# A smaller first sort in single steps, and expert chunks of three, two and three tiles, in a transformer block with mixture of experts

## The chip, the cores and the metric

The kernel runs on one core of a Trainium2 chip. The metric is the device time of one execution in microseconds (us). A core has a tensor engine (PE, with its weight loads PEld), a vector engine (DVE), a scalar engine (ACT), a general engine (POOL) and a sync engine (SP). Each runs its own instructions in order and waits on semaphores; transfers are issued on the queues of SP, ACT and POOL.

## The reference

The input is 8 sequences of 512 tokens with 256 channels. Causal attention with 16 heads of 16 channels is followed by a residual sum and a layer norm, and this by a mixture of 8 experts in which each expert picks tokens, and again by a residual sum and a layer norm. Cut to what matters here:

```python
x = _layernorm(x + attn(x))
# experts: capacity = 512 * 2 / 8 + 1 = 129
scores = softmax(einsum('bsd,ed->bse', x, router_w), axis=-1)
gate_vals, sel_idx = top_k(swapaxes(scores, 1, 2), capacity)   # per sequence and expert
tokens = x[b_idx, sel_idx]
h = gelu(einsum('becd,edh->bech', tokens, w1) + b1)            # 256 -> 1024
y = einsum('bech,ehd->becd', h, w2) + b2                       # 1024 -> 256
out = zeros_like(x).at[b_idx, sel_idx].add(y * gate_vals[..., None])
x = _layernorm(x + out)
```

So each pair of sequence and expert has 129 tokens: 128, which make one tile (numbered as its sequence), and one over. The leftover tokens of all 8 sequences make a tile of 8 rows, called LEFT.

## The kernel before

**Attention.** `steps()` (L105) is one list of stages in an order written out by hand; every engine walks through it and does its own part. It counts iterations i from -3 to 8 (B = 8), each with 40 places (four groups g of ten, place = 10 g + k). Iteration i does the scores and exponentials (`st`) of sequence i; the products for the row maxima (`nat`) run some three quarters of an iteration ahead, those of values (`av`) a quarter behind; projection, layer norm and router logits (`onorm`, `ot`, `proj`, `rstd`, `logit`, `lexp`, `x1`, `score`) run for the sequence before; `qk` and `v` prepare the sequence after next. DVE reduces the `nat` tiles (L522), which go round three PSUM banks, and other stages share two banks (`stage_ps`), so that PE waits for DVE where DVE is late. Iteration 8 holds only the end of sequence 7.

**First sort.** A sequence and an expert are one row of 512 scores. EARLY = 6 sequences give 48 rows. `pick` (PE transposes, DVE copies to `row_pool`, L592) stands at place 1 of iteration 7. `pick_round` (L149) finds the eight largest of each row, their places, and strikes them out: three DVE operations (MAX8 L152, FIND_INDEX8 L153, MATCH_REPLACE8 L155), each waited for by the next. 17 rounds find 129 values. ROUND_AT puts 13 rounds in iteration 7 and 4 in iteration 8, the last at place 16. `picked` (place 17) casts the places to float (L597), transposes them (L738) and adds the sequences' bases (L601); `fetch` on POOL gathers the tokens of expert jobs 0 and 1 (L424). `cut` (iteration 8, places 1 and 12) splits the first expert's two weights in a high part (ACT, L451) and a low part (POOL, L417). The experts' phase begins when all engines have ended attention.

**Experts.** The tiles are grouped in CHUNKS: (0, 1, 2), (3, 4, 5), (6, 7, LEFT), with 384, 384 and 264 columns. A job is an expert and a chunk; there are 24, in the order of JOBS: (0,0), (0,1), (1,0), (1,1), (0,2), (1,2), then expert by expert, and for the last expert chunk 2 first. `expert_steps()` (L794) is again one list for all engines. Iteration q has ten places m: the eight `up` units of job q + 1 (six matmuls each, L1152), and the `down` tiles of job q (24 matmuls each, L1166) at m = 2, 5, 8. ACT makes gelu (L1021) and the high part (L1026), DVE the low part h_lo (L1090; for job 0 POOL, L979). For a down tile DVE makes y in two operations (L1101, L1104), and POOL adds it to `acc` in memory with an indirect transfer (L993). `turn` of job q + 2 (m = 6) transposes gathered tokens (PE L1128, ACT L1012, DVE tt_lo L1064); `fetch` of job q + 3 (m = 5) gathers them (POOL L962). `cut1` and `cut2` split the next expert's weights (ACT L1034, POOL L985): for expert 1 in iteration 0 at m = 3 and 4; for experts 3 to 7 at m = 1 and 4 of the iteration two before their first job.

**Second sort.** The remaining sequences (LATE = 2, 16 rows) are sorted by DVE in 17 rounds over the iterations -1, 0 and 1 (5, 6 and 6 rounds, same `pick_round`); `picked` at (2, 3) makes their token numbers and those of LEFT (L1079, L1081); the gather of job 4 waits for them.

**End.** FINISH lists at which (q, m) a sequence of `acc` is loaded (SP, L942) and normalized (`norm`: DVE L1109 to L1115, POOL L999, L1001). In this list a stage of place m comes ahead of the down of the same place. ACT applies the norm (L1044) and issues the store (L1037).

Of the kernel before, what the change touches and what calls it, by code (L numbers as in the profile page):

```python
# [5 lines left out]
F32 = mybir.dt.float32  # L6
F32R = mybir.dt.float32r
# [7 lines left out]
P = 128  # L15
# [4 lines left out]
KC = C // P  # L20
# [84 lines left out]
def steps():  # L105

    for i in range(-3, B + 1):
# [40 lines left out]

def pick_round(nc, link, pool, best, at, r):  # L149

    src, eight = pool[r % 2], slice(8 * r, 8 * r + 8)
    link(nc.vector.max(best[:, eight], src[:, :]))  # L152
    link(nc.vector.max_index(at[:, eight], best[:, eight], src[:, :]))  # L153
    if r + 1 < ROUNDS:
        link(nc.vector.match_replace(pool[(r + 1) % 2][:, :], best[:, eight], src[:, :], -1.0))  # L155
# [9 lines left out]
def attention(nc, ctx, xt_d, x_d, wqkv_d, wp_d, wpn_d, rw_d, x1_d, acc_d, ident, scores, chosen, w1_d, w2_d, ahead):  # L165
# [328 lines left out]
    def _(dve):  # L494
# [11 lines left out]
        for stage, b, n in steps():  # L506
# [87 lines left out]
            elif stage == "round":  # L594
                pick_round(nc, link, row_pool, best, best_at, n)
                if n == ROUNDS - 1:
                    nc.vector.tensor_copy(best_f[:, :], best_at[:, :]).then_inc(best_ready, 1)  # L597
# [147 lines left out]
CHUNKS = ((0, 1, 2), (3, 4, 5), (6, 7, LEFT))  # L745
NC = len(CHUNKS)
LATE = B - EARLY
# [11 lines left out]
DOWN_AT = (2, 5, 8)  # L759


def rows_of(tile):
    return B if tile == LEFT else P


def job(q):
# [27 lines left out]
def expert_steps():  # L794
# [4 lines left out]
    for q in range(-1, NQ):  # L799
        for m in range(KH + 2):  # L800
# [18 lines left out]
            if q >= 0 and m in DOWN_AT:  # L819
                yield "down", q, m // 3  # L820
# [18 lines left out]
def experts(nc, ctx, x1_d, acc_d, w1_d, b1_d, w2_d, b2_d, out_d, ident, scores, chosen, ahead):  # L839
# [21 lines left out]
    tok = [ahead["tok0"], ahead["tok1"]] + [sb(f"tok{n}", [P, 3, C], F32) for n in range(2, TOK_RING)]  # L861
    tt_hi = sb("tt_hi", [P, TOK_RING, KC, 3 * P], F32R)
    tt_lo = sb("tt_lo", [P, TOK_RING, KC, 3 * P], F32R)
    g = sb("g", [P, G_RING, 3 * P], F32)
    h_hi = sb("h_hi", [P, 2, KH, 3 * P], F32R)
    h_lo = sb("h_lo", [P, 2, KH, 3 * P], F32R)
# [84 lines left out]
    def _(pool):  # L951
# [17 lines left out]
        for stage, q, n in expert_steps():  # L969
            if stage == "fetch":  # L970
                gather(q)
            elif stage == "up" and q < LO_BY_POOL:
# [3 lines left out]
                if q >= 2 and n == 0:  # L976
                    pool.wait_ge(y_done, 3 * (q - 1))
# [8 lines left out]
            elif stage == "down":  # L986
                e, tiles, _ = job(q)
                j = tiles[n]
                pool.wait_ge(y_ready, 3 * q + n + 1)
# [14 lines left out]
    def _(act):  # L1004
        for stage, q, n in expert_steps():
# [7 lines left out]
            elif stage == "up":  # L1013
# [9 lines left out]
                if q >= 2 and n == 0:  # L1023
                    act.wait_ge(y_done, 3 * (q - 1))
                act.wait_ge(g_done, at + 1)
                nc.scalar.activation(h_hi[:, q % 2, n, 0:cols], g[:, at % G_RING, 0:cols], ACT.Copy).then_inc(g_hi, 1)  # L1026
            elif stage in ("cut1", "cut2"):
# [3 lines left out]
                elif q >= 2:  # L1031
                    act.wait_ge(y_done, 3 * (LAST_JOB[q - 2] + 1))
# [18 lines left out]
    def _(dve):  # L1051
# [7 lines left out]
        for stage, q, n in expert_steps():  # L1059
# [22 lines left out]
            elif stage == "up" and q >= LO_BY_POOL:  # L1082
                _, _, cols = job(q)
                at = KH * q + n
                if q >= 2 and n == 0:
                    dve.wait_ge(y_done, 3 * (q - 1))
# [5 lines left out]
            elif stage == "down":  # L1092
                e, tiles, _ = job(q)
                j, at = tiles[n], 3 * q + n
# [23 lines left out]
    def _(pe):  # L1118
        for stage, q, n in expert_steps():
            e, tiles, cols = job(q) if stage in ("turn", "up", "down") else (0, (), 0)  # L1120
            if stage == "turn":
                pe.wait_ge(tok_in[q % TOK_RING], 48 * (q // TOK_RING + 1))
# [32 lines left out]
            elif stage == "down":  # L1155
                at, rows = 3 * q + n, rows_of(tiles[n])
# [14 lines left out]
def build(nc, xt_d, x_d, wqkv_d, wp_d, wpn_d, rw_d, w1_d, b1_d, w2_d, b2_d, out_d):  # L1171
    x1_d = nc.dram_tensor("x1", [B * T, C], F32).ap()
    acc_d = nc.dram_tensor("acc", [B * T, C], F32).ap()
    with ExitStack() as both:
        def sb(name, shape, dt):
# [14 lines left out]
            "tok0": sb("tok0", [P, 3, C], F32),  # L1190
            "tok1": sb("tok1", [P, 3, C], F32),
# [43 lines left out]
```

## Time and profile before

| | before |
|---|---|
| median of 3 runs | 968.44 us (965.9 to 968.86) |
| the profiled execution | 968.14 us, its span 966.2 us |
| PE busy | 833.6 us (86%), 5864 matmuls |
| DVE busy | 649.0 us (67%) |
| ACT busy | 534.6 us (55%) |
| POOL busy | 527.7 us (55%) |
| transfers | 100.51 MB, mean 104 GB/s |

Busy time is what the engine's own instructions cover; it doesn't say what sets the end. The span of the profiled execution is from its first to its last recorded instruction; the time is somewhat longer. "Idle before" is an engine's idle time ahead of a group and what ended it. Waits give who was waited for; "issue" is time in which an engine waited for nothing that the profile shows. The chain that ended last follows the work back from the last instruction. PEclk or the clock column is the share of full speed (2.4 GHz) that TensorE was granted: 1.00 is full, 0.5 the lower level (1.2 GHz), values between are means over a stretch with both. Attention fills the first 493 us or so, the experts the rest.

### The profile page before, as it was taken

The numbers are of one execution on the slowest core, as the hardware profiler recorded it, in microseconds if no ns is written. First come the engines' busy times: TensorE is split into PE (matmuls) and PEld (weight loads), VectorE is DVE, ScalarE is ACT, GpSimd is POOL, SyncE is SP. The second block draws the span as 40 slices with busy tenths as digits, with TensorE's granted clock in tenths as the row PEclk, the third lists the DMA queues.
The fourth block names the chain that finished last, engine by engine and source line by source line (L and its number), as shares of the span: only waits on it lengthen the run. The fifth ranks groups of instructions, "written<-read, shape, count | busy, mean of one in ns | idle before, by whom it ended". The sixth has DMA issues, their size and how long they took to land. (4 is left out here: it accounts for less than half of the span.)

```text
span 966.2 us, 17052 instructions
## 1 busy us (share of the span) xinstructions
PE 833.6 (86%) x5864; PEld 623.9 (65%) x5864; DVE 649.0 (67%) x1985; ACT 534.6 (55%) x1042; POOL 527.7 (55%) x639
## 2 busy tenths in 40 slices
PE   4669999999999999977656899998989899898990
PEld 3434454544545453433356889998989899898990
DVE  4467778787877878999749955555464735547454
ACT  2126667667676766645345345564555556455455
POOL 6336665656565653323645247757375645738343
PEclk9768999999999999988879899999999999999995
DMA  4998778877776869100151324325242332422257
GB/s 142 165 151 134 123 121 144 144 144 143 141 147 112 153 99 205 62 24 20 47 202 53 74 40 82 96 38 137 35 126 45 93 63 47 125 34 35 37 132 250
DMA packets 90101, 100.51 MB, mean 104 GB/s; under 512 B 8736, under 2 KB 83488, under 8 KB 89888
## 3 DMA queue, kind: packets, MB, share of 16 engines
q1 hardware_dynamic: 72560, 77.92, 38.3%
q0 software_dynamic: 12800, 16.92, 10.3%
q10 hardware_dynamic: 4656, 4.59, 1.4%
q8 instruction: 47, 0.77, 0.3%
q14 instruction: 38, 0.31, 0.1%
HBM read 65.38 MB, written 33.62 MB: 102 GB/s over the span
## 5 line engine op out<-in xcount | busy, mean ns | idle before, releaser
L522 DVE CUSTOM_DVE_ANT_0 n_ps<-n_ps,tri 128x512 f32<-128x512 f32 (+3 forms) x512 | 238.8, 519 | 86.0 <-PE n_ps L652 84.3
L438 ACT ACTIVATE pt<-st_ps 128x512 f32<-128x512 f32 x320 | 184.3, 602 | 68.4 <-PE st_ps L637 53.2
L1090 DVE TENSOR_TENSOR h_lo<-g,h_hi 128x384 fp32r<-128x384 f32 (+1 forms) x184 | 132.6, 729 | 125.5 <-ACT h_hi L1026 116.3
L1166 PE MATMUL y_ps<-w_parts,h_hi 128*128 128x256 f32 (+1 forms) x1152 | 212.4, 279 | 0.3 <-ACT h_hi L1026 0.3
L1021 ACT ACTIVATE g<-h_ps,b 128x384 f32<-128x384 f32 (+1 forms) x192 | 104.3, 543 | 193.5 <-PE h_ps L1152 159.3
L1152 PE MATMUL h_ps<-tt_hi,w_parts 128*128 128x384 f32 (+1 forms) x768 | 177.3, 335 | 30.6 <-issue 20.0
L381 POOL TENSOR_SCALAR_AFFINE_SELECT pt<-pt 128x256 f32<-128x256 f32 (+1 forms) x320 | 110.7, 363 | 125.3 <-ACT pt L438 124.5
L1166 PEld LDWEIGHTS y_ps<-w_parts,h_hi 128*128 128x128 f32 (+1 forms) x1152 | 171.6, 177 | 3.6 <-ACT h_hi L1026 0.6
L993 POOL DMA_INDIRECT acc<-y,tok_no x64 | 103.7, 1621 | 114.7 <-DVE y L1104 105.9
L1166 PE MATMUL y_ps<-w_parts,h_lo 128*128 128x256 f32 (+1 forms) x576 | 160.6, 279 | 0.0
L1152 PEld LDWEIGHTS h_ps<-tt_hi,w_parts 128*128 128x128 f32 x768 | 132.2, 198 | 33.4 <-issue 31.8
L637 PE MATMUL st_ps<-w_parts 99*128 99x512 bf16 (+3 forms) x512 | 126.9, 310 | 16.8 <-ACT pt L438 14.8
L652 PE MATMUL n_ps<-w_parts 96*128 96x512 bf16 (+3 forms) x512 | 127.0, 312 | 11.2 <-DVE nmax L522 7.5
L1166 PEld LDWEIGHTS y_ps<-w_parts,h_lo 128*128 128x128 f32 (+1 forms) x576 | 101.8, 177 | 2.0
L637 PEld LDWEIGHTS st_ps<-w_parts 99*128 99x128 bf16 x512 | 41.8, 99 | 89.6 <-ACT pt L438 56.9
L1026 ACT ACTIVATE h_hi<-g 128x384 fp32r<-128x384 f32 (+1 forms) x192 | 94.4, 492 | 7.4
L669 PE MATMUL av_ps<-pt,vaug 128*32 128x512 f32 (+3 forms) x1024 | 97.1, 454 | 1.6 <-POOL pt L381 1.6
L1152 PE MATMUL h_ps<-tt_lo,w_parts 128*128 128x384 f32 (+1 forms) x384 | 95.5, 332 | 0.0
L962 POOL DMA_INDIRECT tok<-x,tok_no x58 | 58.9, 1015 | 33.0 <-DVE left_no L1081 16.4
L985 POOL TENSOR_TENSOR w_parts<-w_raw,w_parts 128x2048 fp32r<-128x2048 f32 x14 | 67.5, 4868 | 12.8 <-ACT w_parts L1034 12.8
L522 DVE DVE_READ_ACCUMULATOR2_ANT nmax<- 128x1 f32 x512 | 72.8, 142 | 0.0
L652 PEld LDWEIGHTS n_ps<-w_parts 96*128 96x128 bf16 x512 | 44.7, 100 | 41.9 <-DVE nmax L522 26.2
(160 smaller groups left out, 1137.6 us busy)
## 6 DMA issues: line engine op xcount, KB each, us to landing
w_parts<-part_d SPq DMA_DIRECT2D x192, 128.0 KB, 6.5
w_raw<-in_w SPq DMA_DIRECT2D x16, 1024.0 KB
part_d<-w_raw SPq DMA_DIRECT2D x96, 128.0 KB, 6.6
w_raw<-in_xt SPq DMA_DIRECT2D x8, 512.0 KB, 4.7
res<-in_x SPq DMA_DIRECT2D x8, 512.0 KB, 10.4
x<-res SPq DMA_DIRECT2D x8, 512.0 KB, 3.3
acc<-res SPq DMA_DIRECT2D x8, 512.0 KB, 4.7
fin<-acc SPq DMA_DIRECT2D x4, 512.0 KB, 4.2
```

What stands on the lines that cost most here:

```text
L381: nc.gpsimd.affine_select(out=x, in_=x, compare_op=ALU.is_ge, fill=0.0, base=0, pattern=[[0, len(tiles)], [1, P]], channel_multiplier=-1). ...
L438: nc.scalar.activation(pt[:, slot % PT_RING, n % UP, :], st_ps[at % ST_RING][:, :], ACT.Exp, scale=S_SCALE).then_inc(exp_done, 1)
L522: ins = nc.vector.tensor_tensor_reduce(out=src[:, h, :], in0=src[:, h, :], in1=mask, scale=-1.0, scalar=-BIG_NEG, op0=ALU.add, op1=ALU.min ...
L637: ins = nc.tensor.matmul(st_ps[at % ST_RING][:, c:c + T - kb * P], kst[0:KM, b % 2, h, kb * P:(kb + 1) * P], qst[0:KM, b % 2, h, kb * P:T] ...
L652: ins = nc.tensor.matmul(bank[:, j * w:(j + 1) * w], qst[0:KQ, b % 2, h, qb * P:(qb + 1) * P], kst[0:KQ, b % 2, h, 0:w], start=True, stop= ...
L669: ins = nc.tensor.matmul(av_ps[VW * j:VW * (j + 1), n * P:T], vaug[:, seq % 3, n, h, :], pt[:, (seq * PAIRS + h // 2) % PT_RING, u, c:c + ...
L993: nc.gpsimd.indirect_dma_start(acc_d[:, :], bass.IndirectOffsetOnAxis(ap=choice(e, j), axis=0), y[0:rows_of(j), j, :], None, compute_op=AL ...
L1021: nc.scalar.activation(g[:, at % G_RING, 0:cols], h_ps[at % H_RING][:, 0:cols], ACT.Gelu, bias=b1[:, e, n:n + 1]).then_inc(g_done, 1)
L1026: nc.scalar.activation(h_hi[:, q % 2, n, 0:cols], g[:, at % G_RING, 0:cols], ACT.Copy).then_inc(g_hi, 1)
L1090: nc.vector.tensor_tensor(h_lo[:, q % 2, n, 0:cols], g[:, at % G_RING, 0:cols], h_hi[:, q % 2, n, 0:cols].bitcast(F32), ALU.subtract).then ...
L1152: ins = nc.tensor.matmul(h_ps[at % H_RING][:, 0:cols], w[e % 2][:, k, units], x[:, q % TOK_RING, k, 0:cols], start=i == 0, stop=i == len(t ...
L1166: ins = nc.tensor.matmul(y_ps[at % Y_RING][0:rows, 0:C], x[:, q % 2, m, toks], w[e % 2][:, m, :], start=i == 0, stop=i == len(terms) - 1)
```

## The change

EARLY falls from 6 to 5: the first sort has 40 rows and can start one iteration earlier, at place 1 of iteration 6. Its 50 operations (the last round needs no strike-out) are no longer placed in rounds of three but one by one (`sort_step`): eight in iteration 6 (every fifth place from 3 on), in iteration 7 one at places 2, 4, 7 and 9 and from place 10 one in each place, two where the place divides by 4. That makes 49; the last one stands at place 9 of iteration 8, where `picked` and `fetch` now are (before: place 17). The `cut` places stay.

The second sort therefore has LATE = 3 sequences, 24 rows. The middle chunk must hold sorted sequences only, so CHUNKS becomes (0, 1, 2), (3, 4), (5, 6, 7, LEFT), with 384, 256 and 392 columns. Downs stand at m = 3, 7 for a chunk of two tiles, at 2, 5, 8 for three and at 1, 4, 7, 9 for four. Waits that counted three tiles per job count with `downs_before` and `gathered`. JOBS, the cuts, the rounds of the second sort, `turn` and `fetch` places stay. FINISH is written anew: sequences 6, 7 and 5 are loaded in the last iteration but one; 3 and 4 come last.

```diff
-EARLY = 6
+EARLY = 5
 ROUNDS = -(-CAP // 8)
 CUTS_AT = ((B, 1), (B, 12))
-ROUND_AT = [(B - 1, place) for place in (1, 2, 8, 11, 12, 16, 17, 23, 25, 26, 32, 38, 39)]
-ROUND_AT += [(B, place) for place in (1, 5, 12, 16)]
+PICKED = (B, 9)
+SORTS = 3 * ROUNDS - 1
+SORT_AT = {(B - 2, place): 1 for place in range(3, 40, 5)}
+SORT_AT.update({(B - 1, place): 1 for place in (2, 4, 7, 9)})
+SORT_AT.update({(B - 1, place): 1 + (place % 4 == 0) for place in range(10, 40)})
...
-                if (i, place) == (B - 1, 1):
+                if (i, place) == (EARLY + 1, 1):
                     yield "pick", 0, 0
-                if (i, place) in ROUND_AT:
-                    yield "round", 0, ROUND_AT.index((i, place))
+                for n in range(SORT_AT.get((i, place), 0)):
+                    if sorts < SORTS:
+                        yield "sort", 0, sorts
+                        sorts += 1
                 if (i, place) in CUTS_AT:
                     yield "cut", 0, CUTS_AT.index((i, place))
-                if (i, place) == (B, 17):
+                if (i, place) == PICKED:
+                    while sorts < SORTS:
+                        yield "sort", 0, sorts
+                        sorts += 1
                     yield "picked", 0, 0
                     yield "fetch", 0, 0
...
+def sort_step(nc, link, pool, best, at, n):
+
+    r, what = n // 3, n % 3
+    src, eight = pool[r % 2], slice(8 * r, 8 * r + 8)
+    if what == 0:
+        link(nc.vector.max(best[:, eight], src[:, :]))
+    elif what == 1:
+        link(nc.vector.max_index(at[:, eight], best[:, eight], src[:, :]))
+    else:
+        link(nc.vector.match_replace(pool[(r + 1) % 2][:, :], best[:, eight], src[:, :], -1.0))
...
-CHUNKS = ((0, 1, 2), (3, 4, 5), (6, 7, LEFT))
+CHUNKS = ((0, 1, 2), (3, 4), (5, 6, 7, LEFT))
...
-DOWN_AT = (2, 5, 8)
+DOWN_AT = {2: (3, 7), 3: (2, 5, 8), 4: (1, 4, 7, 9)}
...
+def downs_before(q):
+
+    return sum(len(CHUNKS[c]) for _, c in JOBS[:q])
...
-FINISH = [((NQ - 2, 0), "load", 6), ((NQ - 2, 1), "load", 7), ((NQ - 2, 4), "norm", 6), ((NQ - 2, 7), "norm", 7),
-          ((NQ - 1, 0), "load", 0), ((NQ - 1, 1), "load", 1), ((NQ - 1, 3), "load", 2), ((NQ - 1, 4), "norm", 0),
-          ((NQ - 1, 5), "load", 3), ((NQ - 1, 8), "load", 4), ((NQ - 1, 9), "load", 5)]
-FINISH += [((NQ - 1, 9), "norm", b) for b in range(1, 6)]
+FINISH = [((NQ - 2, 1), "load", 6), ((NQ - 2, 2), "load", 7), ((NQ - 2, 3), "load", 5), ((NQ - 2, 5), "norm", 6), ((NQ - 2, 7), "norm", 7),
+          ((NQ - 2, 9), "norm", 5), ((NQ - 1, 0), "load", 0), ((NQ - 1, 1), "load", 1), ((NQ - 1, 3), "load", 2), ((NQ - 1, 4), "norm", 0),
+          ((NQ - 1, 5), "norm", 1), ((NQ - 1, 7), "norm", 2), ((NQ - 1, 8), "load", 3), ((NQ - 1, 9), "load", 4)]
+FINISH += [((NQ - 1, 9), "norm", b) for b in (3, 4)]
...
-            if q >= 0 and m in DOWN_AT:
-                yield "down", q, m // 3
+            if q >= 0 and m in DOWN_AT[len(CHUNKS[JOBS[q][1]])]:
+                yield "down", q, DOWN_AT[len(CHUNKS[JOBS[q][1]])].index(m)
```

## Rows read from the trace of the kernel before

**Rows 1.** Busy time by stage: stretch, length, each engine's busy time (x instructions), clock, DMA

```profile
388.00:412.00 24.00, 22.79 (x168) 10.65 (x167) 22.85 (x104) 16.09 (x31) 9.27 (x25) 1.00 0.15 48
...
412.00:453.00 41.00, 31.13 (x203) 13.76 (x201) 37.72 (x120) 19.77 (x36) 12.24 (x33) 0.88 0.04 14
```

**Rows 2.** Waits of PE, 412 to 466 us: who waited for whom, total, times, longest

```profile
PE st_ps L637 <- ACT pt L438: 5.1, 5, 3.4
...
PE n_ps L652 <- DVE nmax L522: 3.2, 2, 1.9
...
PE stage_ps L714 <- DVE nm L555: 1.8, 1, 1.8
```

**Rows 3.** Groups of DVE instructions, 412 to 466 us: busy, mean ns | idle before

```profile
L152 DVE MAX8 best<-row_pool 48x8 f32<-48x512 f32 x15 | 10.2, 682 | 0.3
```

**Rows 4.** Timeline, end of attention: start, length, engine, line, tile, shapes [idle before]

```profile
465.79 9.02 POOL L417 TENSOR_TENSOR w_parts<-w_raw,w_parts 128x2048 fp32r<-128x2048 f32 x2 [1.40 <-ACT w_parts L451]
...
472.73 2.17 DVE L597 CAST best_f<-best_at 48x136 f32<-48x136 uint32 x1
...
482.81 0.94 POOL L424 DMA_INDIRECT tok<-x,tok_no  x1 [0.30 <-issue]
...
483.77 1.06 POOL L410 TENSOR_TENSOR rstd<-ve,half 128x4 f32<-128x4 f32 x1
```

**Rows 5.** Chain that ended last, 490 to 625 us: start, length, what

```profile
522.01 8.35 DVE h_lo L1090
...
554.23 1.15 issue
...
564.66 0.07 DVE left_no L1081
...
570.48 1.11 PE tp_ps L1128 x6
...
623.01 0.99 issue
```

**Rows 6.** Chain that ended last, 636 to 700 us, one expert's period

```profile
642.09 2.16 PE h_ps L1152 x18
...
644.25 2.80 PE y_ps L1166 x24
...
656.93 3.52 issue
...
660.45 4.94 PE h_ps L1152 x18
...
668.19 3.13 PE h_ps L1152 x18
```

**Rows 7.** Timelines of POOL and DVE in that period

```profile
646.56 4.62 POOL L985 TENSOR_TENSOR w_parts<-w_raw,w_parts 128x2048 fp32r<-128x2048 f32 x1 [1.76 <-ACT w_parts L1034]
...
653.79 5.13 POOL L985 TENSOR_TENSOR w_parts<-w_raw,w_parts 128x2048 fp32r<-128x2048 f32 x1
...
653.60 5.48 DVE L1104 TENSOR_SCALAR y<-y,gate 128x256 f32<-128x256 f32 x1
```

**Rows 8.** Chain that ended last, 860 to 967 us

```profile
880.40 2.84 issue
...
917.15 3.13 PE h_ps L1152 x18
...
944.12 6.16 DMA acc<-y,tok_no
...
950.30 6.89 DMA w_raw<-acc
...
957.22 1.42 DVE stats L1109 x4
```

**Rows 9.** All 72 additions: from the instruction's start to landing, from the source view of L993

```profile
DMA to landing us min/median/max: 2.6/3.8/3.9
```

**Rows 10.** The page, part 6: a load of the sum, KB each, median us to landing

```profile
fin<-acc SPq DMA_DIRECT2D x4, 512.0 KB, 4.2
```

More of the change, by code:

```diff
@@ L105, in steps @@
 def steps():
+    sorts = 0
     for i in range(-3, B + 1):
@@ L146, in numbers @@
     return {x: n for n, x in enumerate(x for x in steps() if x[0] in stages)}
-def pick_round(nc, link, pool, best, at, r):
[L151 to L155, printed above, removed]
+def sort_step(nc, link, pool, best, at, n):
[7 more added lines that the diff above has]
+        link(nc.vector.match_replace(pool[(r + 1) % 2][:, :], best[:, eight], src[:, :], -1.0))
+def pick_round(nc, link, pool, best, at, r):
+    for n in range(3 * r, min(3 * r + 3, SORTS)):
+        sort_step(nc, link, pool, best, at, n)
 def weight_parts(ahead, name, slot):
@@ L593, in _ @@
                 dve.wait_ge(dve_free, dve_no[(stage, b, n)] + 1)
-            elif stage == "round":
-                pick_round(nc, link, row_pool, best, best_at, n)
-                if n == ROUNDS - 1:
+            elif stage == "sort":
+                sort_step(nc, link, row_pool, best, best_at, n)
+                if n == SORTS - 1:
                     nc.vector.tensor_copy(best_f[:, :], best_at[:, :]).then_inc(best_ready, 1)
@@ L744 @@
 LEFT = B
-CHUNKS = ((0, 1, 2), (3, 4, 5), (6, 7, LEFT))
+CHUNKS = ((0, 1, 2), (3, 4), (5, 6, 7, LEFT))
 NC = len(CHUNKS)
+TILES = max(len(chunk) for chunk in CHUNKS)
+WIDE = 3 * P + B
 LATE = B - EARLY
@@ L758, with gathered @@
 ROUNDS_IN = (5, 6, 6)
-DOWN_AT = (2, 5, 8)
+DOWN_AT = {2: (3, 7), 3: (2, 5, 8), 4: (1, 4, 7, 9)}
 def rows_of(tile):
     return B if tile == LEFT else P
+def downs_before(q):
+    return sum(len(CHUNKS[c]) for _, c in JOBS[:q])
+def gathered(q):
+    return 16 * sum(len(CHUNKS[JOBS[x][1]]) for x in range(q % TOK_RING, q + 1, TOK_RING))
 def job(q):
@@ L860, in experts @@
     w2_hi, w2_lo = zip(*(weight_parts(ahead, "w2", slot) for slot in range(2)))
[L861 to L866, printed above, removed]
+    tok = [ahead["tok0"], ahead["tok1"]] + [sb(f"tok{n}", [P, TILES, C], F32) for n in range(2, TOK_RING)]
+    tt_hi = sb("tt_hi", [P, TOK_RING, KC, WIDE], F32R)
+    tt_lo = sb("tt_lo", [P, TOK_RING, KC, WIDE], F32R)
+    g = sb("g", [P, G_RING, WIDE], F32)
+    h_hi = sb("h_hi", [P, 2, KH, WIDE], F32R)
+    h_lo = sb("h_lo", [P, 2, KH, WIDE], F32R)
     y = sb("y", [P, B + 1, C], F32)
@@ L976, in _ @@
                 if q >= 2 and n == 0:
-                    pool.wait_ge(y_done, 3 * (q - 1))
+                    pool.wait_ge(y_done, downs_before(q - 1))
                 pool.wait_ge(g_hi, at + 1)
@@ L1023, in _ @@
                 if q >= 2 and n == 0:
-                    act.wait_ge(y_done, 3 * (q - 1))
+                    act.wait_ge(y_done, downs_before(q - 1))
                 act.wait_ge(g_done, at + 1)
@@ L1085, in _ @@
                 if q >= 2 and n == 0:
-                    dve.wait_ge(y_done, 3 * (q - 1))
+                    dve.wait_ge(y_done, downs_before(q - 1))
                 if q == LO_BY_POOL and n == 0:
@@ L1093, in _ @@
                 e, tiles, _ = job(q)
-                j, at = tiles[n], 3 * q + n
+                j, at = tiles[n], downs_before(q) + n
                 rows, before = rows_of(j), sum(j in CHUNKS[c] for _, c in JOBS[:q])
@@ L1121, in _ @@
             if stage == "turn":
-                pe.wait_ge(tok_in[q % TOK_RING], 48 * (q // TOK_RING + 1))
+                pe.wait_ge(tok_in[q % TOK_RING], gathered(q))
                 for k in range(KC):
@@ L1155, in _ @@
             elif stage == "down":
-                at, rows = 3 * q + n, rows_of(tiles[n])
+                at, rows = downs_before(q) + n, rows_of(tiles[n])
                 if n == 0:
@@ L1189, in build @@
             "w2_raw": sb("w2_raw", [P, KH, C], F32),
-            "tok0": sb("tok0", [P, 3, C], F32),
-            "tok1": sb("tok1", [P, 3, C], F32),
+            "tok0": sb("tok0", [P, TILES, C], F32),
+            "tok1": sb("tok1", [P, TILES, C], F32),
             "w1": sb("w1_parts", [P, 2, 2 * KC * HID], F32),
```

4 lines of the change are left out of this document (2 added, 2 removed).

## Prediction

> **What bounds the kernel now.** I read the page first: TensorE is the busiest engine, fuller in the second half (the experts) than around the seam of the two phases. Then busy time by stage. From 388 us on both engines are full: 22.79 us of PE and 22.85 of DVE in 24 us [rows 1]. From 412 to 453 us, where the last sequence is started and the first sort runs, DVE has 37.72 of 41 us, PE only 31.13, at a mean granted clock of 0.88 [rows 1]. PE's waits say for whom: 3.2 us in two waits and 1.8 us in one for DVE directly, and 3.4 us in one wait for an ACT that itself waits for the last router logits, which stand behind sort rounds on DVE [rows 2]. So DVE bounds this stretch. At the seam a chain over DVE and POOL decides: the cast that ends the sort lasts 2.17 us beside the weight cuts on POOL, and the variance step on POOL starts when six gathers are out, at 483.77 us [rows 4].
>
> The chain that ended last tells of the experts. Early on it runs through DVE (the late sort, and one h_lo of 8.35 us beside two cuts) [rows 5]. Later it is PE all the way, broken once in each expert's period: PE stands 3.52 us, and its next 18 matmuls take 4.94 us, not 3.13 [rows 6]. The timelines show why: the second cut (5.13 us on POOL) holds a DVE operation for 5.48 us [rows 7], and the low parts of the next turned tokens are queued behind it. The end is a chain of addition, load, normalization and store, with 6.16 and 6.89 us for the two transfers [rows 8].
>
> **The change, part by part.** I count against the profiled execution: 968.14 us, span 966.2, so 1.9 us lie around the span; it stands 0.3 us under the median of 968.44. One sort step (MAX8, FIND_INDEX8 or MATCH_REPLACE8 with its value load) is about 0.76 us: 682 ns and the gap [rows 3]. I price it alike for 40 and 48 rows, and the late sort alike for 24 and 16, since each partition holds one row.
>
> *Sort in attention.* There are 50 steps either way. Before, 39 stand in the last sequence and 11 behind it; now 8 stand in the sequence before, 41 in the last, 1 behind. Ahead of the last logits, up to where DVE decides, are 8 + 25 steps instead of 30: 3 more, 2.3 us. The copy of the rows (about a step) is moved, not added. The first half of sequence 6 can take some of it; its second half has 1.15 us idle in 24 [rows 1]. Against that, three rounds in the first quarter of the last sequence become four single steps, so DVE's idle 3.3 us in 412 to 453 [rows 1], when it waits for a slowed PE, should mostly go. I take -1.5 us. Bounds: +6.8 (eight steps and the copy all on the path) and -8.4 (all three waits above go [rows 2]).
>
> *Seam.* Ten of the steps behind the last sequence leave the projections' way. What is late next is POOL. The cast now comes beside the first cut, which begins at 465.79 and takes half of 9.02 us [rows 4], so it ends near 470.5; then transposes, and gathers from 471.9; five at 1.25 us to 478.1; then the second cut, now queued behind them, 4.5 us to 482.7; then the variance step, 1.0 us ahead of 483.77 [rows 4]. The last projection's DVE steps may run beside that cut; no row shows their kind there, so the bounds are +3 (held to its end) and -5. The Trainium skill ("SBUF — State Buffer", Who interferes with whom) says that an instruction with at most one SBUF input, outside the two-port modes, is not held by GpSimd. By it the -1.0 stands; if all were held it would be +3. No run yet shows it.
>
> *Start of the experts.* Jobs 0 to 3 are now 3, 2, 3, 2 tiles. DVE has the same 17 rounds in iterations -1 to 1 and still decides; it saves one y in iteration 1 and a third of the columns in two jobs, by estimate three sort steps' worth, 2.2 us. PE's matmuls are equal in sum (1032 columns, nine tiles per expert) but come later: two jobs whose 48 up matmuls take 5.6 instead of 8.35 us (0.117 each, from 2.80 for 24 [rows 6]) and one down of 2.80 us less get done by the end of iteration 2, so 8.3 us of work are left over. Iteration 2 gets no shorter: tiles 5 to 7 and the leftover must be picked before job 4 is gathered. From the leftover's number (564.7) to the transposes (570.48) it took 5.8 us [rows 5]; with a fourth gather it is 7.0, and PE has some 3 us less to do meanwhile. I put 0.1 us. Sum -2.2 + 8.3 + 0.1 = +6.2; bounds +3 (iteration 2 shortens by its work) and +9.
>
> *Second expert's cut.* It falls beside a four-tile job with two downs after the turn, so the 0.99 us stall [rows 5] and 0.2 us of slow clock go: -1.2 (0 if not).
>
> *The cuts of experts 3 to 7.* Both stand in the iteration with the middle chunk's downs and the last chunk's ups. Let it begin at 0 (642.09 us). Before: PE is out of work at 14.8, the second cut starts at 11.7, and PE gets its tokens at 18.4 [rows 6, 7]. After: two ups of 1.065 us (3.13 / 3 for 384 columns [rows 6]) instead of 0.72 stand ahead of the first cut, +0.7. The first down is a place later, behind one more h_lo that this cut holds, and its addition stands ahead of the second cut on POOL: +0.5, of which I keep 0.3. Tokens at 19.4; PE again out of work at 14.8 (8 x 1.065, 0.7 for the turn, 2 x 2.80). The stall grows by 1.0 in four periods. In the fifth, whose stall was 2.84 [rows 8], by 1.7. PE then runs slow: behind 3.52 us of standing that cost 1.8 [rows 6]; I add 0.5 for each, an estimate. Sum 4.0 + 1.7 + 2.5 = +8.2; bounds 0 (no growth) and +13.
>
> *End.* The last job has two tiles and no ups beside it. In DVE's order the normalization of sequence 2 now stands ahead of the last y. Counted from the start of iteration 22: tile 2's matmuls end at 14.0; behind a normalization on DVE and its power step on POOL its addition goes out at 16.9, lands 3.8 us later [rows 9], the load 4.2 later [rows 10], near 25; with 2.1 us of statistics (1.42 of them sums [rows 8]) the last y comes at 27 and its addition at 29.2, though PE ended at 19.6. Then 3.8 to the load, about 5 for it (between 4.2 [rows 10] and 6.89 [rows 8]), 9.0 as before: 47. Before it was 49.05 (from 917.15 [rows 8]), but 5.55 us of PE work have moved ahead of this point: +3.5; bounds -4.3 (DVE doesn't wait) and +7.7 (both transfers as slow as before).
>
> Sum: -1.5 - 1.0 + 6.2 - 1.2 + 8.2 + 3.5 = +14.2, so 968.1 + 14.2 = **982.3 us**.
>
> **The rivals.** (a) *The attention phase gives back more than the rest costs.* For it: single steps are what relieves PE's 8.4 us of waits [rows 2]; the clock of 0.88 goes with them (0.12 of 41 us is 4.9), and the seam gives up to 5. That is -18.3, with nothing lost in sequence 6, against +16.7: 966.5; with the end half way to its bound (-0.4 instead of 3.5) 962.6. It decides for faster from 16.7 us on. Against: 388 to 412 us has no room on DVE [rows 1]. (b) *The cuts and the end don't grow*, because DVE and POOL meet their work in a kinder order: -2.5 + 6.2 - 1.2 = +2.5, 970.6. For it: both terms rest on sums of half microseconds. (c) *Worse:* the longer stalls lower the clock for longer (+4.8, the cuts' bound) and the steps in sequence 6 lie on the path (+3): 990. (d) *The change doesn't do what it says:* the sort does not end earlier where it counts, because the cast waits for a cut and the second cut for the gathers. It is in the sum: the seam gives 1.0 us, not 5.
>
> **How the numbers follow.** The forecast as summed 50%, (a) 17%, (b) 20%, (c) 13%. The likeliest one's own range is 976 to 988. For 8 in 10 I reach half into (a) and to (c): 964 to 990. A measurement of this kernel tells 0.3% (2.9 us) from no change. Faster takes (a), 0.17; within 0.3% about half of (b), 0.12; slower the rest, 0.71.
>
> **What would show it.** Right: the experts begin 1 to 5 us earlier; PE's waits in the last sequence shrink; PE stands about 4 us before the transposes of job 4; stalls of over 4 us once per period, each with a DVE operation held by a cut; the last y some 7 us after PE's last matmul. Wrong: experts that begin over 8 us earlier, stalls of 3.5 us or less, or a last y right behind PE.

## The result, and the profile of the changed kernel

The changed kernel is slower: 992.38 us (median of 4 runs, 991.47 to 994.04) against 968.29 us for the kernel before in the same comparison (965.9 to 968.86). The ratio is 1.025, with an interval of 1.023 to 1.027. The forecast was 982.3 us with a range up to 990.0: right in sign, too small by 10 us, and the time lies outside the range. The profiled execution has a span of 992.0 us (before: 966.2) and a mean granted clock of 0.915 (before: 0.936).

The same two stretches as [rows 1] first. In this execution the clock falls already in sequence 6 (0.86, before 1.00). Over both stretches together PE is busy 55.2 us with 364 matmuls, before it was 53.9 us with 370, so it is busier without doing more:

```profile
388.00:412.00 24.00, 21.47 (x136) 9.58 (x137) 22.45 (x96) 12.99 (x25) 7.42 (x20) 0.86 0.13 45
412.00:453.00 41.00, 33.77 (x232) 14.60 (x230) 36.51 (x123) 22.82 (x41) 13.80 (x38) 0.85 0.06 15
```

PE's waits from 412 to 466 us, as [rows 2]:

```profile
PE st_ps L656 <- ACT pt L457: 5.8, 5, 4.1
PE stage_ps L733 <- DVE nm L574: 2.0, 1, 2.0
...
PE n_ps L671 <- DVE nmax L541: 1.1, 2, 0.6
```

The two direct waits on `nmax` fell from 3.2 to 1.1 us, but the other two that the prediction counts grew, from 3.4 to 4.1 and from 1.8 to 2.0: 7.2 us in all are left of 8.4. Rival (a) lived on their going.

The seam, as [rows 4], timelines of DVE and POOL. The cast takes 0.22 us: it comes just behind the first cut, which ended at 471.19. The second cut comes behind the five gathers, and the variance step follows the last projection's DVE work (L600), not the gathers. The projection's operation with one PSUM and one SBUF input (L587) takes 0.42 us at 480.55, inside the second cut, and 0.42 to 0.43 us in all 32 places of the execution. By the Trainium skill ("SBUF — State Buffer", Who interferes with whom) GpSimd doesn't hold such an instruction; the rows agree, and the bound of +3 falls.

```profile
471.27 0.22 DVE L616 CAST best_f<-best_at 40x136 f32<-40x136 uint32 x1
...
478.00 0.94 POOL L443 DMA_INDIRECT tok<-x,tok_no  x1 [0.30 <-issue]
478.96 4.52 POOL L436 TENSOR_TENSOR w_parts<-w_raw,w_parts 128x2048 fp32r<-128x2048 f32 x1
...
478.73 0.42 DVE L587 SCALAR_TENSOR_TENSOR res<-stage_ps,res 128x256 f32<-128x256 f32 x1 [5.00 <-PE stage_ps L747]
...
480.55 0.42 DVE L587 SCALAR_TENSOR_TENSOR res<-stage_ps,res 128x256 f32<-128x256 f32 x1 [0.93 <-PE stage_ps L747]
...
484.80 1.04 POOL L429 TENSOR_TENSOR rstd<-ve,half 128x4 f32<-128x4 f32 x1 [1.31 <-DVE ve L600]
```

One period of an expert, in the chain that ended last (start, length, what), as [rows 6]:

```profile
647.93 4.31 PE h_ps L1183 x24
652.24 2.83 PE y_ps L1197 x24
...
662.88 4.97 issue
667.85 4.18 PE h_ps L1183 x12
672.03 3.43 PE y_ps L1197 x24
...
706.19 4.31 PE h_ps L1183 x24
```

PE stands 4.97 us, not 3.52; the 12 up and 24 down matmuls behind it take 4.18 and 3.43 us, where the same ones take 2.09 and 2.84 at full clock; and 24 down matmuls in full flow take 2.84 us, not the 2.80 of before. The period is 706.19 - 647.93 = 58.26 us. The timelines of POOL and DVE there, as [rows 7]:

```profile
653.19 4.61 POOL L1016 TENSOR_TENSOR w_parts<-w_raw,w_parts 128x2048 fp32r<-128x2048 f32 x1 [2.55 <-ACT w_parts L1065]
...
654.17 4.54 DVE L1121 TENSOR_TENSOR h_lo<-g,h_hi 128x392 fp32r<-128x392 f32 x2 [2.27 <-ACT h_hi L1057]
...
660.21 6.61 DVE L1121 TENSOR_TENSOR h_lo<-g,h_hi 128x392 fp32r<-128x392 f32 x2 [0.30 <-ACT h_hi L1057]
...
660.81 5.10 POOL L1016 TENSOR_TENSOR w_parts<-w_raw,w_parts 128x2048 fp32r<-128x2048 f32 x1
...
666.75 1.01 DVE L1095 TENSOR_TENSOR tt_lo<-tp_ps,tt_hi 128x384 fp32r<-128x384 f32 x2
```

The iteration starts at 647.93, the second cut 12.9 us later: the low parts of the tokens (666.75) come behind two h_lo that need 6.61 us beside that cut.

The end, first on DVE's timeline:

```profile
970.81 1.41 DVE L1140 BATCH_NORM_STATS2 stats<-w_raw 128x6 f32<-128x256 f32 x4 [1.38 <-DMA w_raw<-acc]
...
972.81 0.42 DVE L1132 TENSOR_TENSOR y<-y_ps,b 128x256 f32<-128x256 f32 x1
```

then in the chain, as [rows 8]:

```profile
964.40 6.39 DMA w_raw<-acc
...
974.84 3.85 DMA acc<-y,tok_no
978.71 4.29 DMA w_raw<-acc
983.02 1.42 DVE stats L1140 x4
```

PE's last matmul starts at 963.22; the last y (972.81) stands behind the normalization of sequence 2, which waited for its load; that landed after 6.39 us.

**Where the 25.8 us of the span are.** I cut both traces at three marks: the first transposes of tokens, the start of iteration 6, and the start of iteration 22 (an iteration starts with its first up matmul).

| stretch | before | after | difference |
|---|---|---|---|
| attention and seam, to the first transposes | 493.34 | 494.34 | +1.00 |
| start of the experts, to iteration 6 | 130.66 | 138.04 | +7.38 |
| iterations 6 to 21 | 293.15 | 311.21 | +18.06 |
| iteration 22 to the end | 49.05 | 48.41 | -0.64 |

The 5.55 us of PE work of the prediction's last term lie in the third stretch instead of the fourth. With them put back, the periods lose 12.5 us and the end 4.9.

### The profile page after: what moved, and what is told of

It reads as the page before. It is cut to its first block, busy times and chain, and to the rows that moved or that the text cites. A ratio compares the mean times of both kernels' runs of the same rounds, so it can differ in the third digit from the quotient of the medians.

```text
span 992.0 us, 17062 instructions
## 1 busy us (share of the span) xinstructions
PE 848.1 (85%) x5864; PEld 634.1 (64%) x5864; DVE 649.1 (65%) x1985; ACT 533.5 (54%) x1042; POOL 525.2 (53%) x639
## 4 chain that ended last, share of the span: by engine, by line
PE 39%; DVE 4%; issue 3%; DMA 2%; ACT 1%; POOL 1%; POOLq 0%; DVEq 0%; ACTq 0%
PE y_ps L1197 19%; PE h_ps L1183 18%; PE tp_ps L1159 2%; DVE h_lo L1121 1%; DMA w_raw<-acc 1%; DMA acc<-y,tok_no 1%; DVE late_best_at L166 1%; DVE late_pool L168 1%; DVE late_best L164 1%; DVE stats L1140 0%; POOL rstd L1030 0%; POOL tok L993 0%; ACT g L1052 0%; DMA tok<-x,left_no 0%; ACT w_raw L1075 0%
## 5 line engine op out<-in xcount | busy, mean ns | idle before, releaser
L1121 DVE TENSOR_TENSOR h_lo<-g,h_hi 128x256 fp32r<-128x256 f32 (+2 forms) x184 | 146.5, 804 | 117.1 <-ACT h_hi L1057 116.9
L1052 ACT ACTIVATE g<-h_ps,b 128x384 f32<-128x384 f32 (+2 forms) x192 | 104.2, 543 | 215.5 <-PE h_ps L1183 215.5
L1197 PE MATMUL y_ps<-w_parts,h_hi 128*128 128x256 f32 (+1 forms) x1152 | 217.5, 283 | 0.7 <-ACT h_hi L1057 0.7
L1183 PE MATMUL h_ps<-tt_hi,w_parts 128*128 128x384 f32 (+2 forms) x768 | 179.3, 338 | 38.7 <-issue 27.1
L1197 PEld LDWEIGHTS y_ps<-w_parts,h_hi 128*128 128x128 f32 (+1 forms) x1152 | 175.1, 180 | 4.4 <-ACT h_hi L1057 0.9
L1197 PE MATMUL y_ps<-w_parts,h_lo 128*128 128x256 f32 (+1 forms) x576 | 162.9, 283 | 0.0
L688 PE MATMUL av_ps<-pt,vaug 128*32 128x512 f32 (+3 forms) x1024 | 101.5, 472 | 1.5 <-POOL pt L400 1.5
L1057 ACT ACTIVATE h_hi<-g 128x384 fp32r<-128x384 f32 (+2 forms) x192 | 94.4, 492 | 7.4
L1183 PE MATMUL h_ps<-tt_lo,w_parts 128*128 128x256 f32 (+2 forms) x384 | 96.2, 333 | 0.0
L993 POOL DMA_INDIRECT tok<-x,tok_no x59 | 59.4, 1007 | 30.4 <-issue 16.6
L1132 DVE TENSOR_TENSOR y<-y_ps,b 128x256 f32<-128x256 f32 (+1 forms) x72 | 30.3, 421 | 67.9 <-PE y_ps L1197 67.7
```

The costliest lines, as they stand in the source:

```text
L688: ins = nc.tensor.matmul(av_ps[VW * j:VW * (j + 1), n * P:T], vaug[:, seq % 3, n, h, :], pt[:, (seq * PAIRS + h // 2) % PT_RING, u, c:c + ...
L1052: nc.scalar.activation(g[:, at % G_RING, 0:cols], h_ps[at % H_RING][:, 0:cols], ACT.Gelu, bias=b1[:, e, n:n + 1]).then_inc(g_done, 1)
L1121: nc.vector.tensor_tensor(h_lo[:, q % 2, n, 0:cols], g[:, at % G_RING, 0:cols], h_hi[:, q % 2, n, 0:cols].bitcast(F32), ALU.subtract).then ...
L1183: ins = nc.tensor.matmul(h_ps[at % H_RING][:, 0:cols], w[e % 2][:, k, units], x[:, q % TOK_RING, k, 0:cols], start=i == 0, stop=i == len(t ...
L1197: ins = nc.tensor.matmul(y_ps[at % Y_RING][0:rows, 0:C], x[:, q % 2, m, toks], w[e % 2][:, m, :], start=i == 0, stop=i == len(terms) - 1)
```

## The experiments

**Is it the sort or the chunks?** Four kernels in one comparison with the kernel before.

The first puts only the sort back in its old order, with five sequences:

```diff
-PICKED = (B, 9)
+PICKED = (B, 17)
...
+SORT_AT = {(B - 1, place): 3 for place in (1, 2, 8, 11, 12, 16, 17, 23, 25, 26, 32, 38, 39)}
+SORT_AT.update({(B, place): 3 for place in (1, 5, 12, 16)})
...
-                if (i, place) == (EARLY + 1, 1):
+                if (i, place) == (B - 1, 1):
```

> The changed kernel (five sequences in the first sort, new chunks, new plan of the end) with the sort's old order: the rows are copied at the start of the last sequence and whole rounds stand at the old places. Only where the sort's operations stand is undone. Theory 1 (nearly all of the loss lies in the experts: start +7, cuts +12, end +5; the sort's place cost about 4 us): some 20 to 22 us above the kernel before, near 989. Theory 2 (the operations in the sequence before the last and the lower clock behind them are the main cost): below 980.

992.11 us, 1.026 of the kernel before (1.024 to 1.028): no difference from the changed kernel. Theory 2 falls; the loss is 25 us, some 3 more than theory 1 has. The second kernel also sets `EARLY = 6`.

> Old sort order and six sequences in the first sort again; only the chunks of 3, 2 and 3 tiles with the leftover, and the new plan of the end, are left of the change. Theory 1 (the chunks cost it by their own form): as the kernel with the old order and five sequences, within 2 us, near 989, because one sequence more or less changes no operation's length. Theory 2 (that the last three sequences are sorted late is what costs at the start of the experts): 5 us or more below that kernel.

990.12 us, ratio 1.023 (1.021 to 1.025). The chunks and the plan of the end alone cost 22 us. In the third no sort step stands in sequence 6 (`pick` moves to sequence 7 as well):

```diff
-SORT_AT = {(B - 2, place): 1 for place in range(3, 40, 5)}
-SORT_AT.update({(B - 1, place): 1 for place in (2, 4, 7, 9)})
-SORT_AT.update({(B - 1, place): 1 + (place % 4 == 0) for place in range(10, 40)})
+SORT_AT = {(B - 1, place): 1 for place in (2, 4, 7, 9)}
+SORT_AT.update({(B - 1, place): 1 + (place % 2 == 0) for place in range(10, 40)})
```

> The changed kernel, but none of the sort's operations stand in the sequence before the last: the rows are copied at the start of the last one and all 50 steps stand there as single steps, two more often than before. Theory 1 (the last sequence is full, so that it doesn't matter in which of the two the steps stand): within 3 us of the changed kernel, 989 to 995. Theory 2 (the eight steps in the sequence before the last lower TensorE's clock from there on): 5 us or more below the changed kernel, 987 or less, with a granted clock of 1.00 from 388 to 412 us.

991.08 us, ratio 1.024 (1.021 to 1.027): it doesn't matter either. Half of theory 2 is borne out: the clock from 388 to 412 us is 1.00 here, as in every trace without steps in sequence 6, while five of the six with them have 0.86 to 0.93. But the 5 us that it promised don't follow, so its price falls. The fourth is the kernel before with those single steps and nothing else:

> The kernel before with the sort alone changed: six sequences, old chunks, old plan of the end, but single sort steps all over the last sequence instead of rounds of three. Theory 1 (single steps save about what they cost): 965 to 972. Theory 2 (rounds of three were what made PE wait in the last sequence, and the chunks took the gain away): 960 or less. Theory 3 (single steps hurt, since they stand between the attention's operations in each quarter): 975 or more.

964.99 us, ratio 0.9972 (0.9959 to 0.9985): single steps give 2.7 us there. In the changed kernel that gain isn't seen: without single steps and with six sequences it takes 990.12 us, with both changes 992.38, and the intervals overlap. So the experts lose nearly all, and what the sort is worth beside them stays open.

**What the cuts cost.** The second cut of experts 3 to 7 goes an iteration later, from place 4 to place 1 of the next; that of expert 2, which the old rule had already put an iteration later, goes from place 4 to place 1 of the same iteration. The edit is the same in the changed kernel and in the kernel before:

```diff
     if stage == "cut1":
         return FIRST_JOB[e] - 2, 1
-    return max(FIRST_JOB[e] - 2, LAST_JOB[e - 2] + 1 if e >= 2 else 0), 4
+    return FIRST_JOB[e] - 1, 1
```

> The changed kernel with one thing moved: of each expert from the third on, the second cut stands at the start of the iteration before the expert's first job, an iteration later than now, so that it no longer comes between the first cut and the turn of the next tokens. Theory 1 (PE's wait once a period is for a DVE that the second cut holds ahead of the turn): the waits of 4.97 us and the slow matmuls behind them (about 2.1 us of up and 1.1 of down matmuls) go in five periods, some 30 to 41 us below the changed kernel, 951 to 962. Theory 2 (two cuts hold DVE for the same time wherever they stand, and the wait only moves): within 5 us of the changed kernel.

> The same move of the second cut in the kernel before. Theory 1: the waits of 3.52 us and about 1.8 us of slow matmuls go in four periods and 2.84 us in the fifth, 20 to 26 us below the kernel before, 942 to 948, and within 12 us of the changed kernel with the same move. Theory 2: within 5 us of the kernel before.

The changed kernel comes to 954.32 us (ratio 0.985, 0.983 to 0.987), the kernel before to **937.79 us** (0.968, 0.965 to 0.970), the fastest version but for the one that adds the single steps (below). The standing is gone in both. The period of the changed kernel with the late cut, in the chain:

```profile
641.63 4.31 PE h_ps L1183 x24
645.94 2.83 PE y_ps L1197 x24
...
658.68 2.84 PE y_ps L1197 x24
661.52 3.15 PE h_ps L1183 x18
...
692.25 4.31 PE h_ps L1183 x24
```

50.62 us instead of 58.26. DVE's timeline in the same period:

```profile
662.01 4.54 DVE L1135 TENSOR_SCALAR y<-y,gate 128x256 f32<-128x256 f32 x1
666.48 1.48 DVE L1121 TENSOR_TENSOR h_lo<-g,h_hi 128x384 fp32r<-128x384 f32 x3
...
671.33 0.74 DVE L1095 TENSOR_TENSOR tt_lo<-tp_ps,tt_hi 128x256 fp32r<-128x256 f32 x2
```

The moved cut (POOL, 4.62 us from 661.78) still holds a DVE operation, for 4.54 us, but DVE has caught up when the next low parts are due. Theory 1 holds in kind for both, with two of its numbers off: the kernel before gained 32 us, not 20 to 26, and the two kernels stand 16.5 us apart, not within 12. The same from the other side: of experts 2 to 7 POOL subtracts only 16 columns of each block,

```diff
-                nc.gpsimd.tensor_tensor(lo[q % 2], raw[:, :, :], hi[q % 2].bitcast(F32), ALU.subtract).then_inc(done, 1)
+                kept = raw.shape[2] if q < 2 else 16
+                nc.gpsimd.tensor_tensor(lo[q % 2][:, :, 0:kept], raw[:, :, 0:kept], hi[q % 2][:, :, 0:kept].bitcast(F32),
+                                        ALU.subtract).then_inc(done, 1)
```

> The changed kernel, but of the experts from the third on POOL subtracts only 16 columns of each block of the weights' low part, the rest is left out. It prices what the cuts on POOL cost through DVE. Theory 1 (the cuts cost the change about 12 us): PE's waits ahead of the transposed tokens go, some 40 us below the changed kernel, near 952, and it stands above the kernel before with the same edit by only 7 to 12 us (start and end of the experts). Theory 2 (the order of the chunks costs it, whatever the cuts do): it stands 20 us or more above that kernel.

> The kernel before with the same part of the cuts left out. Theory 1: its waits of 3.52 us and the slow matmuls behind them go, 20 to 28 us below the kernel before, 940 to 948. Theory 2 (PE would wait there for something else): less than 10 us below.

955.42 us (ratio 0.986) and 937.95 us (0.969): to leave nearly all of POOL's cuts out gives no more than to move one of the two. Without the cuts' effect the new chunks still cost 16.5 us (954.32 - 937.79) and 17.5 (955.42 - 937.95), not the 7 to 12 expected, and not theory 2's 20 either. So the cuts are 6.6 to 7.6 of the 24.1 us; the stretches of the traces with the late cut say where the others are:

| stretch | before, late cut | after, late cut | difference |
|---|---|---|---|
| start of the experts | 131.24 | 137.81 | +6.57 |
| iterations 6 to 21 | 265.30 | 274.34 | +9.04, with 5.55 moved: +3.5 |
| iteration 22 to the end | 47.07 | 48.48 | +1.41, with 5.55 moved: +7.0 |

**The start.** Only 3 of the late sort's 17 rounds are left, and numbers are filled in for the others, so both kernels leave out most of this sort and gather other tokens:

> The changed kernel, but of the late sort's 17 rounds only three are done and numbers are filled in for the others, so that some 32 us of DVE work at the start of the experts are left out. Theory 1 (the smaller jobs of the new chunks lose PE work that this sort used to cover): with the sort gone the changed kernel stands only 15 to 19 us above the kernel before with the same edit, not 24. Theory 2 (what the start loses is lost in PE's waits for tokens and order, not for the sort): still 22 to 26 us above it.

> The kernel before with the same part of the late sort left out. Theory 1: PE's waits at the start of the experts (10.6 us in one) shrink; 10 to 25 us below the kernel before. Theory 2: less than 5 us below it.

981.81 us (ratio 1.014) and 964.31 us (0.995): 17.5 us apart instead of 24. PE's waits from 485 us to iteration 6 in the kernel before with the short sort (who waited for whom, total, times, longest):

```profile
PE h_ps L1158 <- issue: 5.8, 3, 4.6
PE tp_ps L1134 <- DMA tok<-x,left_no: 1.5, 1, 1.5
```

and in the changed kernel with it:

```profile
PE h_ps L1189 <- issue: 5.6, 2, 5.3
PE tp_ps L1165 <- DMA tok<-x,left_no: 3.3, 1, 3.3
```

The wait of 10.6 and 11.5 us for the low parts of tokens behind the sort is gone in both, and the start differs by 130.01 - 126.67 = 3.3 us, not 7.4. That is theory 1: PE work that this sort used to cover now comes after it. But the distance of 17.5 us is theory 1's only in part. From iteration 6 to 21 the kernel before grew by 3.9 us and the changed one by 1.1, which is 2.8 of the 6.6 us by which the two came closer; the added tile lies ahead of the hidden tiles, and 24 down matmuls took 2.87 us in both (see below). And the kernel before gained only 3.6 us, where theory 1 had 10 to 25 and theory 2 under 5: a wait of 4.6 us took the place of the long one, so leaving this sort out buys that kernel little.

**The end.** The normalization of sequence 2 goes behind the last y (in `FINISH`):

```diff
-          ((NQ - 1, 5), "norm", 1), ((NQ - 1, 7), "norm", 2), ((NQ - 1, 8), "load", 3), ((NQ - 1, 9), "load", 4)]
-FINISH += [((NQ - 1, 9), "norm", b) for b in (3, 4)]
+          ((NQ - 1, 5), "norm", 1), ((NQ - 1, 8), "load", 3), ((NQ - 1, 9), "load", 4)]
+FINISH += [((NQ - 1, 9), "norm", b) for b in (2, 3, 4)]
```

> The changed kernel with the normalization of sequence 2 moved on every engine from behind the hidden blocks of the last iteration to behind the last y. Theory 1 (the last y stands 9 to 10 us behind PE because DVE waits for the load of sequence 2 first, and the transfers behind it set the end): the last y goes out right behind PE's last matmul and the end comes 4 to 8 us earlier, 984 to 988. Theory 2 (the additions, loads and normalizations of the last three sequences set the end by themselves, whatever stands ahead of the last y): within 2 us of the changed kernel.

987.35 us, ratio 1.022 (1.018 to 1.025). The chain at the end:

```profile
964.46 6.62 DMA acc<-y,tok_no
971.09 4.13 DMA w_raw<-acc
975.25 1.42 DVE stats L1140 x4
```

The last addition now goes out 6.4 us behind PE's last matmul (958.06), in the changed kernel it was 11.6 us behind; but it lands after 6.62 us instead of 3.85, with two loads of 512 KB in flight until 966.64 and 969.42 us. From iteration 22 to the end it is 45.8 us instead of 48.4: 2.6 of the 4.9 us. That is theory 1 in kind and half in size, and it rests on the traces: by the runs alone the interval overlaps that of the changed kernel (1.023 to 1.027).

**The term that was not in the sum.** With no standing at all a period still takes 50.62 us with the new chunks and 50.02 with the old. First the changed kernel with `WIDE = 400` instead of 392:

> The changed kernel with the rows of the tiles for the turned tokens and the hidden layer padded to 400 columns (1600 bytes) instead of 392 (1568 bytes); nothing else. In the kernels with the second cut moved, whose periods have no standing, a period takes 50.62 us with rows of 392 columns and 50.02 with rows of 384, and 24 down matmuls take 2.84 us instead of 2.80. Theory 1 (the weight load of a down matmul takes longer when a row begins off a 64-byte multiple): 24 down matmuls take 2.80 us again, about 0.04 x 72 = 3 us below the changed kernel. Theory 2 (the three kinds of chunk cost it by their number of columns): no difference in 24 down matmuls.

987.4 us, ratio 1.021 (1.020 to 1.023), some 3 us less than the changed kernel, as theory 1 has it; but 24 down matmuls still take 2.84 us, and from the first transposes to the end it is only 1.3 us less (496.3 against 497.7), so theory 1 as put is not borne out. Then the other way round, on the fast version of the kernel before: rows of `h_hi` and `h_lo` as far apart as in the changed kernel.

```diff
-    h_hi = sb("h_hi", [P, 2, KH, 3 * P], F32R)
-    h_lo = sb("h_lo", [P, 2, KH, 3 * P], F32R)
+    h_hi = sb("h_hi", [P, 2, KH, 3 * P + B], F32R)
+    h_lo = sb("h_lo", [P, 2, KH, 3 * P + B], F32R)
```

> The kernel before with the second cut moved (937.8 us, no standing in its periods of 50.02 us), and the rows of the two tiles of the hidden layer's parts 392 columns apart (1568 bytes) as in the changed kernel, not 384 (1536 bytes): all the work and its order stay. Theory 1 (the row distance makes the weight loads of the down matmuls slower): 24 down matmuls take 2.84 us, not 2.80, a period 50.4, and the kernel 2 to 3 us more. Theory 2 (the distance has no part in it; chunks of 384, 256 and 392 columns are what take longer): 2.80 and 50.02 us as before, within 1 us.

939.23 us (ratio 0.9706, against 0.9679 for that version). The chain, first of the version without the edit, then with it:

```profile
663.03 3.13 PE h_ps L1152 x18
666.16 2.80 PE y_ps L1166 x24
```

```profile
662.18 3.14 PE h_ps L1152 x18
665.32 2.84 PE y_ps L1166 x24
```

The same work in the same order: 2.84 us, a period of 50.48. That is 0.46 of the 0.60 us, from nothing but where the tiles lie; the other 0.14 stay open. Is it the distance of the rows or their place? An unused tile of 32 or of 64 bytes ahead of them, and rows 1600 bytes apart:

```diff
+    sb("pad", [P, 8], F32)
     h_hi = sb("h_hi", [P, 2, KH, 3 * P], F32R)
```

> The kernel before with the second cut moved, and an unused tile of 32 bytes per partition ahead of the two tiles of the hidden layer's parts: rows stay 1536 bytes apart, all of them begin 32 bytes later. With rows 1568 bytes apart, where every second row begins 32 bytes off, 24 down matmuls took 2.84 us. Theory 1 (what counts is whether a row begins at a multiple of 64 bytes): all rows are off, 24 down matmuls take about 2.87 us, a period 50.6 to 50.7, some 4 us more in all. Theory 2 (the distance between rows counts, not where they begin): 2.80 us and 50.02 as before.

> The same with an unused tile of 64 bytes per partition. Theory 1: rows begin at multiples of 64 bytes again, 24 down matmuls take 2.80 us and a period 50.02. Theory 3 (any shift of the tiles against their old place costs, by their place among larger units than 64 bytes): 2.83 us or more.

> The kernel before with the second cut moved, and the rows of the two tiles of the hidden layer's parts 1600 bytes apart (400 columns). Theory 1 (multiples of 64 bytes are enough): 2.80 us for 24 down matmuls and 50.02 us for a period. Theory 3 (only distances like 1536 bytes, a multiple of 512, are free of it): 2.83 us or more, as with 1568 bytes.

944.46 us (ratio 0.976), 939.9 (0.973) and 940.76 (0.972). With 32 bytes, then with 64, then with rows of 1600 bytes, from the chains:

```profile
665.14 3.14 PE h_ps L1153 x18
668.28 2.86 PE y_ps L1167 x24
```

```profile
660.37 3.13 PE h_ps L1153 x18
663.50 2.83 PE y_ps L1167 x24
```

```profile
663.13 3.14 PE h_ps L1152 x18
666.27 2.84 PE y_ps L1166 x24
```

The periods are 50.71, 50.32 and 50.40 us. A shift alone costs, so it isn't the distance only (theory 2 of the first falls); 64 bytes and rows of 1600 bytes don't restore 2.80 us, so multiples of 64 bytes are not enough. 32 bytes cost most. By which unit the place counts stays open. (The tiles allocated behind these two move as well, but PE reads none of them.)

**Do the gains add up?** Single sort steps and the late second cut, six sequences, old chunks:

> Six sequences and the old chunks, with the two edits that gained: single sort steps all over the last sequence, and the second cut an iteration later. Theory 1 (the gains lie in different stages and add up): 2 to 3 us below the kernel with the second cut moved alone, 934 to 936. Theory 2 (what the single steps give is lost again at the start of the experts): 937 to 939.

935.58 us (5 runs, 933.9 to 939.77), ratio 0.968 (0.966 to 0.970): the lowest median, but its ratio is that of the late cut alone, so that an added gain isn't shown. With expert 1's second cut moved as well, `SECOND_AT = ((0, 3), (1, 1))`:

> As the kernel with both edits, and the second cut of expert 1 as well stands an iteration later, so that it no longer lies beside the first and the h_lo operation that takes 8.35 us there. Theory 1 (the two cuts side by side lengthen what PE waits for, 10.6 us ahead of the low parts): PE's wait is 3 to 5 us shorter and the kernel 2 to 5 us faster, 930 to 933. Theory 2 (DVE decides in these iterations by the sum of its work and what is held, wherever the cut stands): within 1.5 us of the kernel with both edits.

938.84 us, ratio 0.969 (0.967 to 0.971). PE's wait for the low parts falls from 10.64 to 6.18 us, but another, 1.05 us a little later, becomes 3.89, and nothing is won. That is theory 2, though the median lies 3.3 us above the kernel with both edits, not within 1.5 (the intervals overlap).

## Why the prediction was right in sign and too small

The step that failed is "PE's matmuls are equal in sum": that term stood at nothing, and it measured 3.5 us in iterations 6 to 21. Without them the time would be 988.9 us, an estimate, and inside the range. The other terms in the experts had the right mechanism, and each was somewhat too small; the first term, of the sort, isn't shown. Rival (c), 990 us, came nearest, but by neither of its causes: the slow matmuls behind the longer waits grew by 2.3 us where the forecast had 2.5, not 4.8 more, and the steps in sequence 6 cost nothing that could be measured.

*Sort in attention and seam (forecast -2.5): not shown in the changed kernel.* For it: the single steps give 2.7 us in the kernel before. And in six executions with the changed attention part (the changed kernel and five experiments that alter only what follows) the experts begin at 485.1 to 494.3 us, on average 490.2; in nine with the old one at 490.3 to 495.6, on average 492.6. The difference is -2.5 (an estimate, with a spread of 9 us over one and the same attention code). The +1.0 of the single pair of profiles lies within that spread. Against it: with the new chunks the kernel with the old sort and six sequences takes 990.12 us, 2 us less than the changed kernel, where the forecast has 2.5 more. As for the steps of the argument, PE's waits moved more than they shrank (7.2 us left of 8.4), and at the seam POOL was indeed relieved, but the variance step then waited for the projection: from the last score matmul to the first transposes it takes 30.8 us in the changed kernel (29.9 to 30.4 in the five experiments) and 30.7 before, so the seam gave some 0.3 us, not 1.0.

*Start of the experts (forecast +6.2 and -1.2): right but for chance.* It measured 7.4, of which 1.6 is chance. From the first transposes to those of job 4 the changed kernel took 75.12 us, not 77.14: 2.0 us less (forecast 2.2 less and 0.1 more). The leftover work was there: between the two kernels with the late cut, 6.57 + 2.2 us come after the transposes of job 4 (forecast 8.3). But the kernel before's own profile was lucky at one place: from the transposes at 570.48 us [rows 5] to the next ones it took 15.64 us, where nine of the ten experiments with the old chunks took 17.2 to 17.4 (the tenth 15.67); in one of them the 24 down matmuls there took 4.14 us, not 2.80, at the slow clock. That puts the typical loss near 5.8. Expert 2's cut did fall away from the path as said (0.99 us of standing).

*The cuts of experts 3 to 7 (forecast +8.2): right, and a term beside them that was missing.* All five waits of the changed kernel sum to 24.2 us, those of before to 17.5: +6.7, where 5.7 was forecast. With the slow clock behind them the effect is the difference between both tables, 12.5 - 3.5 = 9.0 us in the periods, and 6.6 to 7.6 us in the whole kernel by the medians. The failed step shows here: the columns are equal, their time is not. 3.5 us of the periods come with no wait at all, 0.46 of 0.60 us per period from the place of the hidden tiles alone. The prediction took 2.80 us for 24 down matmuls over from before, and had no bound for it.

*End (forecast +3.5): mechanism right, size too small, 4.9, and 7.0 once the cuts are out of the way.* The last y came 9.6 us after PE's last matmul, not 7 to 8, since the load of sequence 2, put at 4.2 us, landed after 6.4 beside other loads; the last load took 4.3, not 5. Half the term is the order of the normalization (2.6 us), the rest is the two transfers, which the order doesn't remove.

In the spans the miss is 25.8 - 14.2 = 11.6 us: attention and seam 3.5, the start 2.4, the unforeseen PE time 3.5, the cuts 0.8, the end 1.4. The medians are 24.1 us apart, so there it is 9.9. Of these, the PE time, the cuts, the end and 0.8 us of the start make 6.5 us that the traces show; the other 3.4 no run locates, and they are about what the forecast had the sort give back. One chance was mis-added: half of rival (b)'s 20% is 10%, not 12.

The largest finding wasn't asked by the change: the second cut's place costs the kernel before 32 us (ratio 0.968), and its price stood in [rows 7] as one operation of 5.48 us; I read it as a stall of 3.52 and did not ask what the kernel would be without it.

## What to carry to other kernels

Where POOL and DVE work on SBUF side by side, what counts is not how long POOL's operation holds DVE but what stands next in DVE's queue: here the same cut one iteration later cost no more than leaving nearly all of the cuts out. A smaller chunk moves PE work out of a stretch that another engine sets, and it has to be paid for later. When a change alters the shape of a tile that PE reads as weights, compare the time of the same matmuls before trusting that the sum of the columns is the sum of the time.

## What the runs showed of the hardware that I had not expected

24 down matmuls of identical shape and operands take 2.80, 2.83, 2.84 or 2.86 us, steadily through a run, with the place of the tile of their weights: old place, 64 bytes on, rows of 1568 or 1600 bytes, 32 bytes on; with a tile of 544 bytes ahead of them (the short late sort) 2.87. From 2.80 to 2.86 the kernel's period goes from 50.02 to 50.71 us. And the same attention code, in six kernels that differ only behind it, lets the experts begin at 485.1 us in one execution and at 494.3 in another, while the experts' part agrees within 1 us (from the first transposes to the end 497.7 us in the changed kernel, 497.5 with the old order of the sort, 497.4 with six sequences too, 498.1 with no steps in sequence 6). Against such a first half, a single pair of profiles can't price a change of 3 us.
